# Block maxima of a local attention: hi and lo rows laid out by one transfer of 128 partitions in place of two of 32

## The reference

```python
q, k, v = proj(hidden, Wq), proj(hidden, Wk), proj(hidden, Wv)   # 16 heads of 16
scores = einsum('bhqd,bhkd->bhqk', q, k) * scale + bias          # allowed: i - 64 < j <= i
attn = softmax(scores, axis=-1)
out = einsum('bhqk,bhkd->bhqd', attn, v)
x = x + out @ Wo
```

## Time and profile before

| | us |
|---|---|
| three runs | 561.37, 562.60, 568.28 |
| median | 562.6 |
| the profiled execution | 568.08 |
| its span, first to last instruction | 566.3 |
| busy in the span: TensorE | 526.6 |
| busy in the span: VectorE | 390.3 |
| busy in the span: ScalarE | 337.2 |

### The profile page before, as it was taken

The page is one execution under the profiler, slowest core; times in us unless marked ns, Lnnn a source line. Parts: engine busy times, 40 slices in busy tenths (PEclk is TensorE's granted clock), DMA queues, the critical chain, the costliest instruction groups (busy, mean ns, idle before and its releaser), DMA issues.

```text
span 566.3 us, 16447 instructions
## 1 busy us (share of the span) xinstructions
PE 526.6 (93%) x5561; PEld 422.5 (75%) x5561; DVE 390.3 (69%) x1207; ACT 337.2 (60%) x776; POOL 227.5 (40%) x419
## 2 busy tenths in 40 slices
PE   7899999899999899999989868889999999989997
PEld 4567877676776687677777546878888887769996
DVE  6566688788788788778767646666666665542764
ACT  4667787776777687677676423316676666551111
POOL 5100112244245335424423426723555555443661
PEclk9899999989999999999998977999999999998999
DMA  6260101311321320321121114777555454425994
GB/s 209 76 189 5 41 9 37 107 47 66 107 88 34 99 87 33 98 88 71 34 80 50 42 69 134 245 227 266 155 156 159 150 159 133 130 86 170 400 399 152
DMA packets 42559, 69.16 MB, mean 122 GB/s; under 512 B 9708, under 2 KB 28655, under 8 KB 42480
## 3 DMA queue, kind: packets, MB, share of 16 engines
q1 hardware_dynamic: 33984, 43.46, 24.3%
q0 software_dynamic: 6480, 17.31, 8.6%
q10 hardware_dynamic: 2016, 7.34, 3.8%
HBM read 36.43 MB, written 32.06 MB: 121 GB/s over the span
## 4 chain that ended last, share of the span: by engine, by line
PE 80%; ACT 7%; DVE 5%; issue 4%; another core or an unknown queue 2%; DMA 0%; POOL 0%; SPq 0%; ACTq 0%; DVEq 0%; POOLq 0%
PE ps L567 40%; PE ps L626 8%; PE ps L656 6%; PE ps L820 5%; PE ps L911 3%; PE ps L665 3%; PE ps L621 3%; PE ps L578 2%; PE ps L642 2%; ACT probs L1015 2%; PE ps L671 2%; PE ps L710 2%; PE ps L928 1%; ACT vm L988 1%
## 5 line engine op out<-in xcount | busy, mean ns | idle before, releaser
L511 POOL DMA_INDIRECT z_slots<-z,slot x64 | 64.5, 1008 | 120.6 <-PE ps L626 100.3
L567 PE MATMUL ps<-wF,wA 128*128 x639 | 105.6, 304 | 1.7 <-DVE wA L1551 1.0
L552 POOL DMA_INDIRECT y_rows<-vm,dest x71 | 69.6, 980 | 72.5 <-issue 37.8
L567 PEld LDWEIGHTS ps<-wF,wA 128*128 128x128 f32 x639 | 85.2, 189 | 14.3 <-issue 6.2
L1221 DVE TRANSPOSE_TENSOR_REDUCE rmax<-ps 128x32 f32<-128x1024 f32 x64 | 79.6, 1244 | 17.9 <-PE ps L626 16.6
L1015 ACT ACTIVATE probs<-ps 128x1024 f32<-128x1024 f32 x64 | 65.6, 1025 | 34.8 <-PE ps L642 33.9
L626 PE MATMUL ps<-bd,kT 64*128 64x256 f32 x512 | 68.9, 391 | 0.0
L567 PE MATMUL ps<-yT,wA 128*128 128x256 f32 x384 | 61.9, 299 | 1.5 <-DVE yT L1194 1.5
L626 PEld LDWEIGHTS ps<-bd,kT 64*128 64x128 f32 x512 | 51.5, 198 | 5.7
L567 PEld LDWEIGHTS ps<-yT,wA 128*128 128x128 f32 x384 | 50.0, 191 | 4.6 <-issue 1.9
L1119 ACT ACTIVATE vt<-ps 128x256 f32<-128x256 f32 x32 | 12.3, 383 | 56.1 <-PE ps L567 56.1
(11 more groups left out here) (200 smaller groups left out, 1138.2 us busy)
## 6 DMA issues: line engine op xcount, KB each, us to landing
z<-z_slots SPq DMA_DIRECT2D x71, 136.0 KB
zT_scratch<-zT SPq DMA_DIRECT2D x16, 512.0 KB
bd<-y_rows SPq DMA_DIRECT2D x8, 512.0 KB, 9.9
out<-xs SPq DMA_DIRECT2D x16, 256.0 KB, 7.6
wraw_of<-wffn SPq DMA_DIRECT2D x10, 384.0 KB
xs<-x SPq DMA_DIRECT2D x7, 512.0 KB, 4.6
wA<-zT_scratch ACTq DMA_DIRECT2D x7, 512.0 KB, 6.9
z<-y_rows SPq DMA_DIRECT2D x4, 512.0 KB, 10.8
```

The lines of the kernel that those rows point to most:

```text
L511: eng.indirect_dma_start(z_slots, bass.IndirectOffsetOnAxis(ap=slot[:, c, j, t:t + 1], axis=0), z[:, c, t, :], None, bounds_check=E * REGI ...
L552: eng.indirect_dma_start(y_rows, bass.IndirectOffsetOnAxis(ap=dest[:, m:m + 1], axis=0), yo[:, m, :], None, bounds_check=K * T - 1, oob_is ...
L567: mm = eng.matmul(out, lhsT(a), rhs(b), start=start and n == 0, stop=stop and n == 2, skip_group_check=skip)
```

## The change

`rmax` keeps its size, but the 32 maxima of a partition are written in two pieces, those of the first bank to columns 0 to 15 and those of the second to columns 64 to 79. The same transpose then puts the first bank's chunks on partitions 0 to 15 and the second's on 64 to 79. `neg_max` reduces all 128 partitions into one tile `neg` [128, 2, 32]; partitions whose columns of `rmax` are zero give zero. The lo part is written by two operations, from partitions 0 to 31 onto 32 to 63 and from 64 to 95 onto 96 to 127, over the upper halves of the zeros there. `neg` then has, by partitions of 16: hi of bank 0, zeros, lo of bank 0, zeros, hi of bank 1, zeros, lo of bank 1, zeros. One transfer lays this out on every 16th row of `shift`, 8 rows of 16 pieces. It waits for both lo operations. `negm`, `neglo` and the memset of `neglo` are gone, and the shift matmul waits for 16 in place of 32.

```diff
-        negm = sb("negm", [32, 2, 32])
-        neglo = sb("neglo", [32, 2, 32])
-        negmb, neglob = (n[:, :, :].bitcast(BF16).rearrange("p a (c two) -> p a c two", two=2) for n in (negm, neglo))
+        rmax_by_bank = rmax[:, :, :].rearrange("p b (m r) -> p b m r", m=2)
+        neg = sb("neg", [P, 2, 32])
+        negb = neg[:, :, :].bitcast(BF16).rearrange("p a (c two) -> p a c two", two=2)
...
                 def load_mrow(b, pb):
-                    for part, (ready, rows) in enumerate(((s_nm, negm), (s_nl, neglo))):
-                        eng.wait_ge(ready, b + 1)
-                        eng.dma_start(shift[32 * part:P:64, pb, :].rearrange("m (a c) -> m a c", c=32),
-                                      rows[:, pb, :]).then_inc(s_mr[pb], 16)
+                    eng.wait_ge(s_nl, 2 * (b + 1))
+                    eng.dma_start(shift[0:P:16, pb, :].rearrange("m (a c) -> m a c", c=32), neg[:, pb, :]).then_inc(s_mr[pb], 16)
...
-                chain(eng.memset(neglo[:, :, :], 0.0))
...
                 def shift_of(b, g, n):
-                    eng.wait_ge(s_mr[n % 2], 32 * (2 * g + n // 2 + 1))
+                    eng.wait_ge(s_mr[n % 2], 16 * (2 * g + n // 2 + 1))
...
                     eng.wait_ge(s_S, b + 1)
-                    eng.tensor_reduce(rmax[:, n % 2, 0:32], S[n % 2].rearrange("p a (c q) -> p (a c) q", q=32), AX.X,
+                    eng.tensor_reduce(rmax_by_bank[:, n % 2, :, 0:16], S[n % 2].rearrange("p a (c q) -> p (a c) q", q=32), AX.X,
                                       ALU.max, apply_transpose=True).then_inc(s_R, 1)
...
                     eng.wait_ge(s_RT, b + 1)
-                    eng.tensor_reduce(negm[:, n % 2, :], ps[0:32, RT, 0:P].rearrange("p (g q) -> p q g", g=4), AX.X,
+                    eng.tensor_reduce(neg[:, n % 2, :], ps[:, RT, 0:P].rearrange("p (g q) -> p q g", g=4), AX.X,
                                       ALU.max, negate=True).then_inc(s_nm, 1)
                     eng.wait_ge(s_nm, b + 1)
-                    eng.tensor_tensor(neglob[:, n % 2, :, 1], negm[:, n % 2, :], negmb[:, n % 2, :, 1],
-                                      ALU.subtract).then_inc(s_nl, 1)
+                    for m in (0, 64):
+                        eng.tensor_tensor(negb[m + 32:m + 64, n % 2, :, 1], neg[m:m + 32, n % 2, :], negb[m:m + 32, n % 2, :, 1],
+                                          ALU.subtract).then_inc(s_nl, 1)
```

## The result

The changed kernel takes 575.47 us (median of four runs, 573.48 to 578.94) against 563.98 us of the kernel before, timed beside it (four runs, 561.37 to 568.28). The ratio is 1.0229, with an interval of 1.0175 to 1.0283. That is 11.5 us by the medians. The ratio leaves out the kernel before's execution of 568.28 us, a slower one than the rest and the one that was profiled, and gives 12.9 us, from 562.60. The forecast was 8.2 us slower, 571 us, within 566 to 575; the measured median lies 0.5 us above that, inside the wide range (562 to 576), and over the line of 2% to which the forecast gave 0.16.

A forecast was written before the change was run, and what follows sets the result against it. TensorE is the bound, VectorE matters only where TensorE waits for it. Late o costs 5.1 + 1.2 + 0.2 + 0.7 + 0.5 + 0.5 = 8.2 us on 562.6, so 571 us, forecast 566 to 575, wide range 562 to 576.

The forecast's parts named there:

- the line of 2%: Whole kernel: over 2% slower means above 573.9 us, from late transfer and part of the forecast's upper end; chance 0.16.
- the rows land 0.10 us earlier: Transfer to the shift matmul: the single issue comes 0.46 us after neg instead of 0.56, so rows land 0.10 earlier.
- the sum: Attention stage: delays of o added over all turns, 5.1 + 1.2 + 0.2 + 0.7 + 0.5 + 0.5 = 8.2 us.
- The two lo operations: VectorE between neg and o: both steps wait for the end of the one ahead, 0.31 us more in all.
- Reductions on 128 partitions cost nothing: VectorE's reduction to the negated maxima: 128 partitions in place of 32 add nothing.
- The pair n = 3 and n = 0: End of a turn: TensorE 0.15 us late in n=3, 0.51 in all after n=0; ten pairs cost 5.1 us.
- The engine count of the forecast: The merged transfer: 8 engines in place of 2, each again carrying 16 pieces.
- it lands as fast: The merged transfer of 128 pieces: with 16 pieces on each engine it takes no longer to land than before.
- Not slower: Rival, VectorE: the lo operations overlap, only 0.11 us more, so 563 us, range 560 to 565; chance 0.25.
- The late transfer: Rival, rows of maxima: the transfer stays on 2 engines and lands 0.61 us later, 581 us; chance 0.10.
- The chain n = 3 to n = 0: Forecast: VectorE carries n=3's delay into n=0; rival without carrying: 0.31 a pair, 568 us, counted with the forecast.
- Nothing changed behind the attention stage: Rest of the kernel after the last shift matmul: no change, nothing there gives the loss back.

The follow-up runs named there:

- e1: Kernel before with its lo operation split into two of 16 columns on the same partitions, second transfer waiting for both: ratio 1.0013.
- e2: Kernel before plus an unused second lo operation on other partitions, second transfer waiting for both: ratio 1.0177, and 1.0157 in the third set.
- e5: Changed kernel plus a third, unused lo operation from partitions 0-31 onto 32-63, which the transfer awaits: 1.0417 of the kernel before.
- hi only: Lo operations left out: changed (wide) layout 0.9870 and 0.9920 of the kernel before; the kernel before so cut (narrow) 0.9876, 0.9952 and 0.9865.
- e10: Changed kernel with reciprocal and o moved ahead of the two lo operations: 1.0896 of the kernel before, fourth set alone.
- e6: Changed kernel with eight unused small matmuls on TensorE ahead of o's transpose in steps n = 3: 1.0216 of the kernel before.
- e4: Kernel before without its lo operation and second transfer, first set: ratio 0.9876.
- e4b: Kernel before without its lo operation and second transfer, run again in the third set: ratio 0.9952.
- e4c: Kernel before without its lo operation and second transfer, run again in the fourth set: ratio 0.9865.

## Why the prediction was right or wrong

In short: the mechanism held, and the size was missed. The step that failed is "the rows land 0.10 us earlier", which was to give back part of the delay: they land some 0.08 us later. Besides, the sum had no term for turns with a lowered clock.

**Bound and mechanism: right.** TensorE waits less for the rows and more for o, in steps n = 3 (0.46, where the results of TensorE come late) and n = 0 (0.19), each as named. Shown by e1 against e2, and by e5's dose.

**The two lo operations: right in kind, 0.05 short.** Forecast 0.31 us more on VectorE, measured 0.36 (1.30 against 0.94). The operations are 0.22 apart, and the reciprocal, which no longer overlaps the operation ahead, is 207 ns instead of 191; the reduction to `neg` is 290 instead of 278 ns. "Reductions on 128 partitions cost nothing" was wrong by that 12 ns and no more.

**An undisturbed turn: 0.53 forecast, 0.55 from the second lo operation alone (e2), 0.73 in all.** The steps, by medians of the undisturbed turns, grew by 0.44 (n = 0 to 1), 0.06, 0.12 and 0.12 us (n = 3 to 0), 0.73 in all but for rounding. The pair n = 3 and n = 0 is 0.56, where the forecast had 0.15 + 0.36, so it was close. The other two steps together are 0.18, where it had 0.02 in most turns. In e2 the same four are 0.43, 0.10, 0.01 and 0.01: the agreement of its 0.55 with the forecast's 0.53 is partly luck, since the 0.15 of n = 3 isn't there and 0.10 stands in a step that the forecast left out. What the changed kernel has beyond e2 lies in n = 2 to 3 and n = 3 to 0.

**"The rows land 0.10 us earlier": the step that failed.** The issue came 0.76 us after neg's start instead of 0.84, so only 0.08 earlier, since the reduction took longer. But the wide transfer doesn't land as fast: from issue to the shift matmul's load it is at best 1.81 us, in the earlier trace rows it was 1.67, and at best 1.64 in others. Neg's start to that load is then 2.57 us at best and 2.60 by the median of all blocks; before, the median was 2.52. So the rows are 0.08 us later, where the forecast had them 0.10 earlier. The engine count of the forecast holds: a window of 2 us in the changed kernel with one transfer has these packets on the queue,

```profile
q1 hardware_dynamic: 136, 0.02, 5.3%
```

128 pieces and 8 more, where 64 pieces had 4 more; by the forecast's reading that is 8 engines with 16 pieces each. The price lay elsewhere, in 0.10 us more of issue and some 0.06 more of landing, which the sum put at nothing: the rows' start was worked out from the operations alone, and "it lands as fast" from the pieces for each engine. Beside e2 it is 0.17 us a turn, about 2 us in all. That split rests on the turns of one profile each; by the times, 1.0229 against 1.0177, and 1.0178 against 1.0157, the intervals overlap, and with hi only the difference was -0.1 and 0.55%. So that the second lo operation is the main cause is shown; the transfer's share is not shown to better than that.

**The sum, in the profiled executions.** The fifteen turns grew from 300.4 to 313.6 us. The first gave 0.94 (forecast 0.5), the next three 0.34, 0.50 and 0.47 (1.3 together, forecast 1.2), eleven turns 0.73 each (8.0, where the forecast had 5.1 for the pairs and 0.9 for n = 2), and 3.0 are left over: turns with a lowered clock, seven instead of four. These are four falls of the clock to 0.50, its lower level, against two, since most of them lie across the edge of a turn; each costs some 1.6 to 1.7 us. The forecast had no term for the clock. The numbers compare one execution with one, and another pair would differ. In e10 a granted clock of 0.50 came with idle stretches of 2.1 us. In the changed kernel it fell at 139.2, 204.1, 289.4 and 333.8 us, each 1.7 to 2.0 us after one of the late starts of `neg`; TensorE then waits 0.37 us for o, but it does so in all eleven steps n = 3, and in seven the clock stayed. e1 has the late starts and 0.08 us of that wait, and no such fall in its eleven turns; the kernel before has none of the wait and two. So the clock term is open: no run changed the idle time alone, and e6 couldn't settle it. In the second set, with neither late starts nor, to speak of, a lowered clock, the change costs 1.6 to 2.0%, near the forecast's 1.5; beside the result it is 2.3 (1.75 to 2.83), and the intervals overlap.

**The rivals.** Not slower fell with e2's chain: no overlap. The late transfer fell with 136 packets and with 1.81 us to the matmul, where it had 2.3. The chain n = 3 to n = 0 carries the delay. "Nothing changed behind the attention stage" can't be told finer than the scatter of 219 to 226 us there in these sets.

**The side of 2%.** With 8.2 us forecast and 11 as the line, 2 or 3 us of small terms decided it, and all the terms that were left out (issue, landing, longer reduction and reciprocal, clock) had one sign. A chance of 0.16 on that side was too low.

## What to carry to other kernels

Before merging small transfers, look at what the merge asks of the engine that feeds them: an operation on another group of partitions, with the one behind it held too, cost 0.35 us here where splitting one on the same partitions cost 0.07, and the transfer saved had been hidden. Where one engine has two ways out to the bound engine, measure the slack of both, since shifting work from one to the other can lose far more than it may win (9% in e10, though part of that goes with the late results of its set; 1.2 to 1.4 us in turns of 19 without them). When one turn is read for a forecast, ask of each long wait in it whether the program explains it: the 1.31 us before neg in the earlier trace rows belonged to the set and not to the kernel. And when every term left out of a sum has the same sign, move the range that way.

## What the runs showed of the hardware

- A transfer of 128 pieces of 128 bytes on 8 rows holds SP's queue 597 ns, one of 32 pieces on 2 rows 496 ns; the load of the waiting matmul starts at best 1.81 us after the first's issue begins and 1.64 after the second's.
- The reciprocal takes some 190 ns when it overlaps the lo operation ahead (e1) and 207 to 208 ns when it starts behind the end of the operation ahead: behind a change of partitions (e2), but also behind an idle stretch with the same partitions (208 ns in e4).
- The same kernel on the same chip took 534 us in one set and 563 in the next. The clock isn't the main reason: the narrow hi-only kernel's turns from the fifth on took 18.5 to 18.9 us in the third set (e4b) and 19.7 to 20.2 in the fourth (e4c), all at the granted clock 1.00, and its first four turns were alike. In the fourth, `neg` started 1.2 us after its matmul's end in every step n = 3 from the fifth turn on, in the third never over 0.6. The stage behind the last shift matmul took 225.0 against 215.3 us. Why was not found.
